# A gated attention block with a routed feed-forward: the first five token steps in a written order of their own

## What is computed

```python
x = x + tanh(g_xattn[0]) * xattn(layernorm(x), ctx, W, b)   # x: 8 x 256 x 256, ctx: 8 x 120 x 256
x = x + tanh(g_ffn[0]) * ffn(layernorm(x), expert_sel, keys, values)
# xattn: q = x @ W.T + b; softmax(q @ ctx.T) @ ctx
# ffn: the 4 best of 64 experts by sigmoid(x @ expert_sel.T);
#      sum over them of gate * relu(x @ keys[e]) @ values[e]      (256 -> 128 -> 256)
```

## Time and profile before

| | |
|---|---|
| median of 3 runs | 307.73 us (306.81 to 308.65) |
| span of the profiled execution, first to last instruction | 254.5 us |
| TensorE busy | 191.2 us (75%) |
| GpSimd busy | 139.4 us (55%) |
| VectorE busy | 132.4 us (52%) |
| ScalarE busy | 109.4 us (43%) |
| moved by DMA | 66.01 MB, 259 GB/s |

### The profile page before, as it was taken

The page is one execution under the profiler, slowest core; times in us unless marked ns, Lnnn a source line. Parts: engine busy times, 40 slices in busy tenths (PEclk is TensorE's granted clock), DMA queues, the critical chain, the costliest instruction groups (busy, mean ns, idle before and its releaser), DMA issues.

```text
span 254.5 us, 4511 instructions
## 1 busy us (share of the span) xinstructions
PE 191.2 (75%) x1316; PEld 146.4 (58%) x1316; DVE 132.4 (52%) x496; ACT 109.4 (43%) x307; POOL 139.4 (55%) x156
## 2 busy tenths in 40 slices
PE   7866996976976832207999999999999994009873
PEld 6744764654744521004888888887878771007752
DVE  3657268897688877200122222356666552506584
ACT  2555287867686741000345454454555551000111
POOL 4004254777777777760367777777777777700000
PEclk9995699997999655555899999999999998555999
DMA  6999999999999999993769976676666422169996
GB/s 159 239 290 320 358 336 331 343 376 320 329 316 301 284 298 314 337 312 95 223 202 332 333 202 211 195 237 163 186 210 200 132 78 83 62 222 408 385 417 236
DMA packets 40894, 66.01 MB, mean 259 GB/s; under 512 B 5381, under 2 KB 24603, under 8 KB 40864
## 3 DMA queue, kind: packets, MB, share of 16 engines
q1 hardware_dynamic: 32572, 46.68, 60.3%
q0 software_dynamic: 6624, 16.82, 19.1%
q10 hardware_dynamic: 1668, 2.17, 2.3%
HBM read 38.31 MB, written 28.64 MB: 263 GB/s over the span
## 4 chain that ended last, share of the span: by engine, by line
PE 51%; DMA 12%; DVE 11%; POOL 8%; ACT 7%; issue 7%; POOLq 1%; SPq 1%; DVEq 0%; ACTq 0%
PE bank L735 13%; PE bank L764 11%; DMA keys_sb<-y_rows 10%; POOL x_slots L525 7%; PE bank L729 6%; PE bank L567 4%; PE bank L657 2%; PE bank L770 2%; PE bank L754 2%; DMA x_slots<-rows,pos_i 2%; DVE xs L1107 2%; PE bank L620 1%; PE bank L779 1%; PE bank L663 1%; PE bank L672 1%
## 5 line engine op out<-in xcount | busy, mean ns | idle before, releaser
L535 POOL DMA_INDIRECT y_rows<-rows,by_place x74 | 73.5, 993 | 35.8 <-issue 20.4
L525 POOL DMA_INDIRECT x_slots<-rows,pos_i x64 | 63.0, 984 | 46.3 <-DVE pos_i L1090 23.8
L987 ACT COPY xT<-bank 128x512 f32<-128x512 f32 (+1 forms) x38 | 21.8, 575 | 55.7 <-PE bank L729 54.0
L1235 DVE TENSOR_SCALAR shared<-bank 128x256 f32<-128x256 f32 (+1 forms) x38 | 15.9, 418 | 52.6 <-PE bank L735 42.8
L735 PE MATMUL bank<-xT,keys_sb 128*128 128x128 f32 x256 | 38.2, 290 | 0.4 <-ACT xT L987 0.3
L735 PEld LDWEIGHTS bank<-xT,keys_sb 128*128 128x128 f32 x256 | 32.4, 194 | 8.2 <-ACT xT L987 5.7
L764 PE MATMUL bank<-values_sb,shared 128*128 128x256 f32 x128 | 34.4, 385 | 0.2 <-DVE shared L1235 0.2
L1001 ACT COPY rows<-bank 128x512 f32<-128x512 f32 (+1 forms) x38 | 21.8, 576 | 15.3 <-PE bank L764 11.6
L1310 DVE SCALAR_TENSOR_TENSOR xs<-keys_sb,by_place,xs 128x256 f32<-128x256 f32 x36 | 15.6, 481 | 16.7 <-DMA keys_sb<-y_rows 16.3
L764 PEld LDWEIGHTS bank<-values_sb,shared 128*128 128x128 f32 x128 | 21.4, 190 | 3.8 <-issue 2.1
L729 PE MATMUL bank<-ident,rows 128*128 128x128 f32 x148 | 22.5, 277 | 0.0
(11 more groups left out here) (145 smaller groups left out, 314.5 us busy)
## 6 DMA issues: line engine op xcount, KB each, us to landing
x_slots<-values_sb SPq DMA_DIRECT2D x4, 2056.0 KB
rows<-x_slots SPq DMA_DIRECT2D x64, 128.5 KB, 3.6
keys_sb<-y_rows SPq DMA_DIRECT2D x16, 512.0 KB, 5.8
values_sb<-in_L_ffn_values SPq DMA_DIRECT2D x5, 1024.0 KB, 13.5
xs<-in_x SPq DMA_DIRECT2D x8, 256.0 KB, 8.6
out<-xs ACTq DMA_DIRECT2D x7, 256.0 KB, 6.1
values_sb<-in_L_ffn_values SPq DMA_DIRECT2D x1, 1408.0 KB, 27.4
rows<-x_slots SPq DMA_DIRECT2D x40, 32.1 KB
```

Source lines behind the costliest of these rows:

```text
L525: pool.indirect_dma_start(x_slots, bass.IndirectOffsetOnAxis(ap=pos_i[:, t * K + k:t * K + k + 1].bitcast(U32), axis=0), rows[:, t % RB * ...
L535: pool.indirect_dma_start(y_rows, bass.IndirectOffsetOnAxis(ap=result_at[:, t:t + 1], axis=0), y_sb[:, t % R, :], None, bounds_check=last_ ...
L987: act.copy(xgT[:, 2 * ring + part.start:2 * ring + part.stop, :].rearrange("p u d -> p (u d)"), pT(place_of(part, ring))[:, part.start * D ...
L1235: dve.tensor_scalar(hidT[:, 2 * ring + part.start:2 * ring + part.stop, :].rearrange("p u n -> p (u n)"), pH(place_of(part, ring))[:, part ...
```

## The change

The helpers stay as they are, but for three waits. On TensorE, ScalarE and VectorE the special cases for tiles 0 and 1 go out of the loop, and the calls of the first five steps are written out one by one, with those of the context units 0 to 2 between them; the loop starts at s = 5 and keeps its order. `x_T(t)` now waits for ScalarE's copy of the tile before, `scores(t)` for the copy of `own_dot` of the tile before, and `context_S(0)` for the copy of the bias. The wait for all constants stands ahead of `ranks(0)` on TensorE and ahead of `choose(0)` on VectorE. SyncE and GpSimd are not changed.

```diff
--- before.py
+++ after.py
@@ -281,18 +281,8 @@
             return next(n for n, (first, last) in enumerate(groups) if first <= t < last)
-        CONTEXT_T = {1: 1, 4: 2, 8: 3}
-        CONTEXT_M = {0: 1, 2: 2, 5: 3, 9: 4}
-        CONTEXT_BS = {1: 1, 3: 2, 6: 3, 10: 4}
-        STAT_T = {1: 1, 3: 2, 6: 3, 10: 4}
-
-        def ahead(t):
-
-            return 0 <= t < 2
-
-        def placed_in(s):
-
-            return [t for t in (s - 3, s - 2) if live(t) and ahead(t) == (t == s - 2)]
+        FIRST = 5
+        CONTEXT_T, CONTEXT_M, CONTEXT_BS, STAT_T = {8: 3}, {5: 3, 9: 4}, {6: 3, 10: 4}, {6: 3, 10: 4}
         def kind_of(t):
             return "e" if t < ALONE else MIXED[t - ALONE] if t < TILES else "q"
@@ -595,6 +585,7 @@
             def x_T(t):
                 if t % TB == 0:
                     pe.wait_ge(x_in[t // TB], 16)
+                after(pe, a_Tc, t)
                 for c in range(C):
                     mm = pe.transpose(pX[:, c * P:(c + 1) * P], xs[:, t, c * P:(c + 1) * P], ident[:])
                 mm.then_inc(a_T, 1)
@@ -618,24 +609,6 @@
             for n in range(8):
                 pe.matmul(bank[:, 6, 0:P], ident[:], ident[:], start=True, stop=True)
-            context_T(0)
-            pe.wait_ge(bq_in, 16)
-            pe.transpose(pBq, bq_rows[:], ident[0:C, 0:C]).then_inc(bq_T, 1)
-            pe.wait_ge(sel_ok, 1)
-            pe.wait_ge(bq_ok, 1)
...
-            pe.wait_ge(consts_ok, CONSTS)
-
             def ranks(t):
                 pe.wait_ge(b_hot, t + 1)
                 if t == 0:
@@ -651,6 +624,7 @@
                 if t == 2 * TB:
                     pe.wait_ge(selT_ok, 2)
                 pe.wait_ge(a_Tc, t + 1)
+                after(pe, b_own, t)
                 if t == units[unit_of_batch(b)][0] * TB:
                     pe.wait_ge(c_Mc, unit_of_batch(b) + 1)
                 for c in range(C):
@@ -671,33 +645,73 @@
                 after(pe, b_u, t)
                 pe.matmul(pO, probsT[:, t % 2, :], ctx_sb[:, b, :], start=True, stop=True).then_inc(a_O, 1)
-            for s in range(T + 3):
-                for t in placed_in(s):
-                    if ahead(t):
-                        ranks(t)
-                t = s - 1
...
-                    if not ahead(t):
-                        ranks(t)
+            def probs_T(t):
+                pe.wait_ge(a_exp, t + 1)
+                pe.transpose(pPT, probs[:, t % 2, :], ident[:]).then_inc(a_PT, 1)
+            pe.wait_ge(bq_in, 16)
+            pe.transpose(pBq, bq_rows[:], ident[0:C, 0:C]).then_inc(bq_T, 1)
+            context_T(0)
+            x_T(0)
+            pe.wait_ge(sel_ok, 1)
+            pe.wait_ge(bq_ok, 1)
+            for c in range(C):
+                mm = pe.transpose(pSel[:, c * E:(c + 1) * E], sel_sb[:, c * P:(c + 1) * P], ident[0:E, 0:E])
+            mm.then_inc(sel_T, 1)
+            pe.wait_ge(wq_in, 16)
+            context_M(0)
+            x_T(1)
+            pe.wait_ge(selT_ok, 1)
+            pe.wait_ge(wsum_ok, 1)
+            context_B(0)
+            stat_T(0)
+            scores(0)
+            context_M(1)
+            pe.wait_ge(c_Bc, 1)
+            context_S(0)
+            x_T(2)
+            probs_T(0)
+            scores(1)
+            attended(0)
+            stat_T(1)
+            context_B(1)
+            context_S(1)
+            scores(2)
+            probs_T(1)
+            context_T(1)
+            x_T(3)
+            attended(1)
+            probs_T(2)
+            pe.wait_ge(consts_ok, CONSTS)
+            ranks(0)
+            x_T(4)
+            scores(3)
+            attended(2)
+            context_M(2)
+            context_B(2)
+            context_S(2)
+            probs_T(3)
+            ranks(1)
+            stat_T(2)
+            attended(3)
+            scores(4)
+            x_T(5)
+            context_T(2)
+            for s in range(FIRST, T + 3):
+                if live(s - 1):
+                    probs_T(s - 1)
+                if live(s - 3):
+                    ranks(s - 3)
                 if live(s):
                     scores(s)
-                t = s - 1
-                if live(t) and not ahead(t):
-                    attended(t)
+                if live(s - 1):
+                    attended(s - 1)
                 if live(s + 1):
                     x_T(s + 1)
-
                 if s in CONTEXT_M:
                     context_M(CONTEXT_M[s])
-                if s in CONTEXT_BS and s > 1:
+                if s in CONTEXT_BS:
                     context_B(CONTEXT_BS[s])
                     context_S(CONTEXT_BS[s])
                 if s in STAT_T:
@@ -895,22 +909,6 @@
                 act.wait_ge(a_T, t + 1)
                 act.copy(xT[:, t % 2, :], pX).then_inc(a_Tc, 1)
-            context_T(0)
-            act.wait_ge(bq_T, 1)
-            act.copy(col_sb[:, :, 1:2], pBq.rearrange("p (c a) -> p c a", a=1)).then_inc(bq_ok, 1)
-            act.wait_ge(sel_T, 1)
-            act.copy(m_sb[:, :, 0:2, M:MS],
...
-            act.activation(gate_exp[:], gates_in[:], ACT.Exp, scale=2.0).then_inc(g_exp, 1)
-
             def chances(t):
                 act.wait_ge(b_u, t + 1)
                 act.wait_ge(b_rstd, t + 1)
@@ -932,51 +930,94 @@
                 act.wait_ge(b_ln, t + 1)
                 act.activation(rstd2[:, t:t + 1], ln2[:, t:t + 1], ACT.Exp, scale=-0.5).then_inc(b_rstd, 1)
-            for s in range(T + 3):
-                t = s - 2
-                if live(t):
-                    if ahead(t):
-                        row_copies(t)
-                    else:
-                        chances(t)
-
+            def exponentials(t):
+                act.wait_ge(a_max, t + 1)
+                act.activation(probs[:, t % 2, :], pS[:, 0:M], ACT.Exp, bias=neg_max[:, t:t + 1],
+                               scale=rstd1[:, t:t + 1], accum_out=row_sum[:, t:t + 1]).then_inc(a_exp, 1)
+                act.copy(own_dot[:, t % 2, :], pS[:, M:MS]).then_inc(b_own, 1)
+            def probs_T(t):
+                act.wait_ge(a_PT, t + 1)
+                act.activation(probsT[:, t % 2, :], pPT, ACT.Identity,
+                               scale=gate_tanh[0:M, 0:1]).then_inc(a_PTc, 1)
+            act.wait_ge(bq_T, 1)
+            act.copy(col_sb[:, :, 1:2], pBq.rearrange("p (c a) -> p c a", a=1)).then_inc(bq_ok, 1)
+            context_T(0)
+            x_T(0)
+            act.wait_ge(sel_T, 1)
+            act.copy(m_sb[:, :, 0:2, M:MS],
+                     pSel.rearrange("p (c a e) -> p c a e", c=C, a=1).broadcast_to([P, C, 2, E])).then_inc(selT_ok, 1)
+            act.wait_ge(consts_ok, CONSTS)
+            deviation(0)
+            context_M(0)
+            context_B(0)
+            stat_T(0)
+            x_T(1)
+            act.wait_ge(g_in, 32)
+            act.activation(gate_exp[:], gates_in[:], ACT.Exp, scale=2.0).then_inc(g_exp, 1)
+            deviation(1)
+            exponentials(0)
+            context_S(0)
+            x_T(2)
+            act.wait_ge(tanh_ok, 1)
+            probs_T(0)
+            exponentials(1)
+            context_M(1)
+            stat_T(1)
+            context_B(1)
+            context_S(1)
+            deviation_behind(0)
+            chances(0)
+            probs_T(1)
+            exponentials(2)
+            x_T(3)
+            context_T(1)
+            probs_T(2)
+            row_copies(0)
+            deviation_behind(1)
+            chances(1)
+            row_copies(1)
+            x_T(4)
+            deviation(2)
+            exponentials(3)
+            deviation_behind(2)
+            context_M(2)
+            probs_T(3)
+            chances(2)
+            context_B(2)
+            context_S(2)
+            stat_T(2)
+            row_copies(2)
+            x_T(5)
+            exponentials(4)
+            deviation_behind(3)
+            context_T(2)
+            for s in range(FIRST, T + 3):
+                if live(s - 2):
+                    chances(s - 2)
                 if s - 1 in CONTEXT_BS:
                     context_B(CONTEXT_BS[s - 1])
                     context_S(CONTEXT_BS[s - 1])
                 if s - 1 in STAT_T:
                     stat_T(STAT_T[s - 1])
-                t = s - 1
-                if live(t):
-                    act.wait_ge(a_PT, t + 1)
-                    if t == 0:
-                        act.wait_ge(tanh_ok, 1)
...
-                                   scale=rstd1[:, t:t + 1], accum_out=row_sum[:, t:t + 1]).then_inc(a_exp, 1)
-                    act.copy(own_dot[:, t % 2, :], pS[:, M:MS]).then_inc(b_own, 1)
+                if live(s - 1):
+                    probs_T(s - 1)
+                if live(s - 2):
+                    row_copies(s - 2)
+                if live(s):
+                    exponentials(s)
                 if live(s + 1):
                     x_T(s + 1)
                 if s - 1 in CONTEXT_M:
                     context_M(CONTEXT_M[s - 1])
                 if s - 1 in CONTEXT_T:
```

(106 more changed lines are left out.)

71 lines of the change are left out of this document (removed).

## The result

The changed kernel took 298.14 us, median of 5 runs (294.76 to 301.9), against 307.73 us (305.33 to 311.47, 5 runs) before: ratio 0.9689, 95% interval 0.9593 to 0.9785.

A forecast was written before the change was run, and what follows sets the result against it. GpSimd's unbroken scatter queue from tile 2 on was taken to bound the start of TensorE's expert stage. Tile 2 starts 7.9 us sooner, landing and row loads leave 3.9: 307.73 to 303.8 us, range 299.5 to 306.6.

The forecast's parts named there:

- the sum: Whole kernel: span 254.5 less 3.9 gives 250.6 us; with 53.2 us around the span unchanged, 303.8 us; chance 0.60.
- forecast of 3.9 us: First transpose of expert rows: moves from 120.0 to 116.1 us, and the expert stage behind it moves along.
- landing 4.09 to 7.1: GpSimd's last scatter: issue to landing grows from 4.09 to 7.1 us, as SyncE's queue of keys is still draining.
- all of it passes: Rival: last scatter lands in 4.1 us, rows not held behind the keys; 299.8 us, down to 299.0; chance 0.12.
- `highest(2)`: VectorE's highest score of tile 2: starts at 17.5 us instead of 23.50, as TensorE's idle stretches and other work ahead go.
- From there to tile 2's first scatter: VectorE's list, 13.7 us, plus 1.3 us of handing over, then 0.79 us until GpSimd starts at 33.3 instead of 41.16.
- Granted clock in 10 to 30: TensorE's opening: granted clock stays at 1.00 across 10 to 30 us, where it had fallen to 0.50 from 20.
- Scatters to the last: GpSimd's queue from tile 2's first scatter: no pause, 70.84 us, last scatter at 104.1, 7.9 us sooner.
- Warming matmuls end: TensorE's four warming matmuls (L779): 0.14 and 3.75 us after the last scatter lands at 111.2, so 115.1 us.
- The row loads behind the keys: SyncE's first expert row loads: held behind keys draining until 113.8; first transpose between 115.1 and 116.7, taken as 116.1 us.
- The clock rival: TensorE's opening: clock falls between 17 and 27 or so, tile 2 starts at 36.9; gain 2.3 us, 305.4 us; chance 0.16.
- Slower: Rival: TensorE at half clock from the first scores on, tile 2's scatters start at 44.7; 311.2 us; chance 0.04.

## Why the prediction was right or wrong

**The step that failed** is in the sum: "53.2 us lie around the span, and I leave these unchanged". In every execution with both numbers, 1.7 to 3.0 us lie around it (255.21 and 252.7; 250.97 and 248.9; 301.05 and 299.3). The 53 us were lost inside the executions of the other level, which the shown trace was not of: their spans are 304.1 and 299.3, and taken together without their overlaps the pauses of these two cover 60 and 66 us. A span of 254.5 beside a median of 307.73 was in plain sight in the profile's table, and I explained it away.

**What it cost.** The forecast of 3.9 us holds for the level of the shown trace: 4.1 us measured there, 5.5 on the other such chip. At the level of the timed runs the term "landing 4.09 to 7.1" was wrong: GpSimd is not busy without a break, the last scatter starts 18 to 19 us later, and the keys are no longer in its way (2.65 us from its start to the warming matmuls). With that the 3 to 4 us stay that the sum gave back. The result the sum would then have had, 7.9 us or more, is the rival "all of it passes", which I gave 0.12, for the wrong reason: I weighed it by the keys' bytes and not by when the last scatter starts. That the measured 9.6 us is this lead fits the pairs of traces (4.6 to 9.3 us at the first transpose) but is argued, not shown.

**Step by step, without pauses** (forecast; measured in after): `highest(2)` 17.5; 18.27. From there to tile 2's first scatter 15.8; 15.85. Tile 2 33.3; 34.12, with no pause behind it. Granted clock in 10 to 30 1.00; 1.00. Scatters to the last, 70.8; 70.7. Last scatter 104.1; 104.83. Landing 7.1; 6.00. Warming matmuls end 115.1; 114.7. All of these hold within 1.1 us, so here the mechanism was right. The added waits were not tested by themselves.

**The row loads behind the keys** were mis-sized. I put 2.9 us from a drain's end at 113.8 and took 116.1. SyncE issued the first load at 111.02, VectorE used its rows at 114.12, 3.1 us later, although the DMA share in 112:116 was still 0.92. The warming matmuls set the first transpose (114.72), near the low end of my bounds (115.1); I forecast 116.1. That the gain came out at 4.1 us beside 3.9 is in part luck: the transpose was 1.4 us sooner than forecast, and the before of that comparison 1.0 us sooner than in the shown trace (118.96 and 119.98).

**The landing** was, without pauses, the right term with the right cause: with the keys moved it is 3.08 us, whereas moving them in before changes nothing at the first transpose.

**The clock rival** didn't come about in after, at either level (1.00 through 10 to 35). One group less in the written order, and it does.

**Slower** was ruled out for the right reason: its condition, half clock from the first scores on, was not met.

## What to carry to other kernels

Compare the span of the trace with the timed median before anything else. Here 1.7 to 3.0 us lay between the two for every run with both numbers; 53 us meant that the trace was of another behaviour than the one that was timed, and a sum made on it gives the gain at its own level only. A lead won early can be lost to what was queued for the old schedule: here a bulk load took back 3.5 of 7.7 us, and to cut it up behind the loads that are waited for looked worth about 2 us more (249.3 and 250.9, intervals that overlap). And where a hand-written order fills TensorE's gaps, look at the granted clock beside the order: by my reading about half of what one moved group of six matmuls did to tile 2 came through the clock.

## What the runs showed of the hardware

The same kernel before, text and inputs, takes 253.6 to 261.4 us on two chips and 297 to 312 on three others, with nearly the same busy times of VectorE, ScalarE and GpSimd (132.1, 109.4 and 139.3 us against 131.2, 109.4 and 139.6) and TensorE at 189.7 against 210.8. The slower traces, and only they, have pauses of up to 7.2 us, many of them in about the same places of the program from run to run, at the full granted clock (61 us in after) and at half (112 us), each ended by an instruction that reads a TensorE result. In the traces of the two kernels they are 12 and 13 on VectorE and 17 and 15 on ScalarE. Packets of instructions don't account for them: of the 26 in after that last 1 us or more, none fell into 21. Neither what makes them nor why some chips (or times) have them was found.
